# Shared expert and dispatch of a two-layer attention and mixture-of-experts kernel: which TensorE instruction carries the semaphore update of a finished group

## The reference

```python
scores = softmax(xt @ Wg.T)                       # 16 experts
# best 2 of 4 groups of experts, then the best 4 experts of a row
h = silu(einsum('td,eid->eti', xt, W1)) * einsum('td,eid->eti', xt, W3)   # 176 inner
y = einsum('etd,te->td', einsum('eti,edi->etd', h, W2), combine)
z = silu(xt @ Ws1.T) * (xt @ Ws3.T) @ Ws2.T       # shared expert, 352 inner
x = x + y + z
```

## Time and profile before

| | us |
|---|---|
| median of 3 runs | 1459.74 (1458.84 to 1463.13) |
| profiled execution, first to last instruction | 1458.9 |
| PE busy, of the span | 1153.4 (79%) |
| DVE busy | 873.6 (60%) |
| POOL busy | 689.3 (47%) |
| ACT busy | 543.1 (37%) |
| first stage of shared expert and dispatch, about | 386 to 524 |
| the same of the second layer, about | 1096 to 1237 |

### The profile page before, as it was taken

The page is one execution under the profiler, slowest core; times in us unless marked ns, Lnnn a source line. Parts: engine busy times, 40 slices in busy tenths (PEclk is TensorE's granted clock), DMA queues, the critical chain, the costliest instruction groups (busy, mean ns, idle before and its releaser), DMA issues.

```text
span 1458.9 us, 25835 instructions
## 1 busy us (share of the span) xinstructions
PE 1153.4 (79%) x8690; PEld 619.8 (42%) x8690; DVE 873.6 (60%) x2061; ACT 543.1 (37%) x846; POOL 689.3 (47%) x841
## 2 busy tenths in 40 slices
PE   6878999887862399999468899998788227999990
PEld 2333334334631256665244344443275114666650
DVE  5688899853740135555389799998478002455543
ACT  2226677686400012222122477777841001222210
POOL 4443345442067216677563354444502760467771
PEclk9978999999895699999789899999988658999995
DMA  4325556304522148888655321221071322688868
GB/s 150 116 80 180 180 181 191 119 17 147 151 93 106 68 118 152 146 153 147 126 176 166 119 56 55 57 56 32 24 246 38 108 93 78 141 149 150 154 98 248
DMA packets 154353, 177.42 MB, mean 122 GB/s; under 512 B 20016, under 2 KB 139760, under 8 KB 153712
## 3 DMA queue, kind: packets, MB, share of 16 engines
q1 hardware_dynamic: 124336, 136.38, 31.3%
q0 software_dynamic: 29184, 38.36, 15.5%
q10 hardware_dynamic: 704, 1.02, 0.2%
HBM read 91.12 MB, written 83.78 MB: 120 GB/s over the span
## 4 chain that ended last, share of the span: by engine, by line
PE 55%; DVE 18%; another core or an unknown queue 7%; issue 7%; ACT 5%; DMA 4%; SPq 3%; POOL 1%; POOLq 0%; ACTq 0%; DVEq 0%
PE pair_ps L1963 11%; PE o_ps L1734 7%; DVE nm L1103 4%; PE pair_ps L1996 4%; ACT arena L829 3%; DVE bm L1103 3%; PE pair_ps L1999 2%; PE pair_ps L1906 2%; PE t_ps L1760 2%; PE pair_ps L1684 2%; PE pair_ps L1565 2%; PE pair_ps L1970 2%; DMA arena<-mT 2%; PE pair_ps L1659 2%
## 5 line engine op out<-in xcount | busy, mean ns | idle before, releaser
L829 ACT ACTIVATE arena<-pair_ps 128x1024 f32<-128x1024 f32 x320 | 323.4, 1024 | 137.4 <-PE pair_ps L1659 80.2
L614 POOL TENSOR_SCALAR_AFFINE_SELECT arena<-arena 128x512 f32<-128x512 f32 (+1 forms) x320 | 175.7, 549 | 249.0 <-ACT arena L829 248.5
L1103 DVE TENSOR_REDUCE nm<-pair_ps 128x2 f32<-128x1024 f32 (+1 forms) x192 | 232.6, 1222 | 40.4 <-PE pair_ps L1708 36.9
L672 POOL DMA_INDIRECT x_slots<-y_sb,slot_i x128 | 123.3, 963 | 154.0 <-DVE slot_i L1310 115.6
L1734 PE MATMUL o_ps<-arena 128*9 128x512 f32 (+7 forms) x2048 | 179.5, 446 | 4.3 <-POOL arena L614 4.1
L688 POOL DMA_INDIRECT y_h<-xnT,dest x80 | 124.7, 1559 | 107.6 <-DVE xnT L1453 83.6
L688 POOL DMA_INDIRECT y_f<-xnT,dest x80 | 125.0, 1562 | 105.5 <-DVE xnT L1453 80.4
L1963 PE MATMUL pair_ps<-arena 128*128 x512 | 167.0, 467 | 3.1 <-issue 1.7
L1103 DVE TENSOR_REDUCE bm<-pair_ps 128x8 f32<-128x1024 f32 x128 | 155.3, 1217 | 5.7 <-PE pair_ps L1708 2.7
L1916 PE MATMUL t_ps<-arena,hw 128*128 128x256 f32 (+1 forms) x96 | 30.2, 443 | 123.4 <-DVE x_sb L1399 77.5
L1436 DVE TENSOR_TENSOR arena<-arena,pair_ps 128x128 f32<-128x128 f32 x144 | 41.5, 288 | 127.4 <-ACT arena L885 88.1
(11 more groups left out here) (273 smaller groups left out, 2078.5 us busy)
## 6 DMA issues: line engine op xcount, KB each, us to landing
arena<-x_slots SPq DMA_DIRECT2D x128, 132.5 KB
arena<-in_w SPq DMA_DIRECT2D x4, 2816.0 KB, 18.8
x_slots<-hw SPq DMA_DIRECT2D x19, 530.0 KB, 3.6
arena<-q_a SPq DMA_DIRECT2D x64, 96.0 KB
arena<-q_b SPq DMA_DIRECT2D x64, 96.0 KB
y_f<-hw SPq DMA_DIRECT2D x11, 512.0 KB, 4.1
y_h<-hw SPq DMA_DIRECT2D x11, 512.0 KB, 4.1
arena<-in_w SPq DMA_DIRECT2D x2, 2048.0 KB, 17.1
```

What stands on the lines that cost most here:

```text
L614: pool.affine_select(p, p, pattern, ALU.is_ge, 0.0, base=0, channel_multiplier=-1)\
L672: pool.indirect_dma_start(x_slots, bass.IndirectOffsetOnAxis(ap=slot_i[:, t, k:k + 1], axis=0), y_sb[:, t, :], None).then_inc(sm("scat0" i ...
L829: act.activation(p_ring[:, U % RING, :], pair_ps[:, pair_at("T", n, u)].rearrange("p a c -> p (a c)"), ACT.Exp, scale=SCALE).then_inc(sm(" ...
L1103: dve.tensor_reduce(dst, src, X, ALU.max, negate=not 2 <= u < 4).then_inc(sm("t_max_done"), 1)
```

## The change

At four places of `pe_ffn` the semaphore update is taken off the last matmul of a group and put on a drain instruction that is issued right behind it on the same engine: `scan`, `spread`, `shared_in` and `shared_out`. A drain waits until its engine has finished what was issued ahead of it, and makes its update then. That is 12 + 12 + 1 + 1 = 26 drains in each mixture of experts, 52 in all. No product, wait, value or place in an engine's list changes otherwise. `counts`, whose code stands between these, keeps its update on the matmul, and so do the experts.

```diff
             def scan():
                 pe.wait_ge(sm("e_full"), 1 + past(f, 1))
-                pe.matmul(s_ps[:, 1, 0:1], upper, full[:], start=True, stop=True, skip_group_check=True)\
-                    .then_inc(sm("e_scan"), 1)
+                pe.matmul(s_ps[:, 1, 0:1], upper, full[:], start=True, stop=True, skip_group_check=True)
+                pe.drain().then_inc(sm("e_scan"), 1)
...
                 pe.matmul(ps[:, :, NJ:NP], ones, place1[:, :, MIXED:2 * MIXED], start=False, stop=True,
-                          skip_group_check=True)\
-                    .then_inc(sm("e_spread"), 1)
+                          skip_group_check=True)
+                pe.drain().then_inc(sm("e_spread"), 1)
...
             def shared_in(k):
...
-                        mm = pe.matmul(st_ps[0:m, k % 2, 512 * a:512 * a + 512], ws13[:, a, e, r:r + m],
-                                       xnT_all[:, e, b * T:(b + 1) * T], start=e == 0, stop=e == CE - 1)
-                mm.then_inc(sm("e_h"), 1)
+                        pe.matmul(st_ps[0:m, k % 2, 512 * a:512 * a + 512], ws13[:, a, e, r:r + m],
+                                  xnT_all[:, e, b * T:(b + 1) * T], start=e == 0, stop=e == CE - 1)
+                pe.drain().then_inc(sm("e_h"), 1)
...
             def shared_out(k):
...
-                    mm = pe.matmul((t_ps if u < 2 else o_ps)[:, (u % 2) * E:(u % 2) * E + E],
-                                   hw[0:m, k % 2, u * P:(u + 1) * P], ws2[0:m, c, :],
-                                   start=c == 0 and u % 2 == 0, stop=c == 2, skip_group_check=True)
-                mm.then_inc(sm(f + "_hw_used"), 1)
+                    pe.matmul((t_ps if u < 2 else o_ps)[:, (u % 2) * E:(u % 2) * E + E],
+                              hw[0:m, k % 2, u * P:(u + 1) * P], ws2[0:m, c, :],
+                              start=c == 0 and u % 2 == 0, stop=c == 2, skip_group_check=True)
+                pe.drain().then_inc(sm(f + "_hw_used"), 1)
```

## The result

The changed kernel takes **1473.23 us** (median of 3 runs, 1472.01 to 1475.13) against 1459.74 before: ratio 1.0084, 95% interval 1.0058 to 1.0111. It is slower by 0.8%, above the range's upper end of 1470. Its profiled execution has a span of 1473.4 us, 14.5 more than before, at nearly the same mean granted clock (0.901 against 0.898).

What follows compares the result with a forecast made beforehand. PE's semaphore updates, late under POOL's scatters, were taken to bound the kernel. Gains of 34 and 36 us in the two layers, 70 us, off the profiled 1458.9 give 1388.9, forecast as 1390 with the median 0.8 above; range 1345 to 1470.

Steps and rivals of the forecast that it cites:

- What bounds the kernel: Dispatch: PE's updates come up to 67.1 us late under POOL's scatters, leaving 25.9 us of shared expert before the experts.
- everything prompt: Rival: the experts' updates are not held either, so experts start 58 us early in each layer; 1347, chance 0.12.
- The price of a drain: Between PE's matmul groups, a drain costs 0.35 us: a matmul tail of 0.16 plus a weight load of 0.19.
- If a drain's update arrives promptly, nothing holds PE at 426.67: After spread in the first layer, PE runs on and ends the shared expert by 464 with drains, under the scatters.
- The main case: Shared expert hidden under the scatters, experts start 34 and 36 us earlier in the two layers: 70 us, 1390, chance 0.50.
- half: Rival: drains prompter but not prompt, part of the leftover shared expert stays behind the scatters; half of 70, 1425, chance 0.12.
- Drains hold PE: Rival: each drain stops PE until its late update leaves, 9.4 us a layer plus some 4 for clock; 1483, chance 0.11.
- Drains change nothing in the timing, and cost: Rival: updates stay as late, ten drains a layer stand in the open behind the scatters, 7 us; 1467, chance 0.15.

Runs made afterwards that it cites:

- e14: Kernel before, with POOL waiting after every eighth scatter until all so far have landed; chip with late completions: 1376.57 us, ratio 0.9406.
- e16: Kernel before, with POOL pausing after every 16th scatter only; chip with late completions: 1433.43 us, ratio 0.981.
- e17: Kernel before, with POOL pausing after every 12th scatter; chip with late completions: 1402.64 us, ratio 0.960.
- e13: Kernel before, with drains only behind the last product of scan and of spread, two a layer; chip with late completions: 1465.03 us, ratio 1.0016.
- e12: Kernel before, with drains only behind shared_in 8 to 11 and shared_out 6 to 11, ten a layer; chip with late completions: 1468.58 us, ratio 1.0033.
- e11: The changed kernel with all 52 drains, measured again against the kernel before; chip with late completions: 1475.79 us, ratio 1.0075.
- e9: Kernel before, with drains only behind scan and spread; chip with prompt completions: 1342.12 us, ratio 1.0004.
- e1: Kernel before, with drains only behind scan and spread, four in the run; chip with prompt completions: 1341.33 us, ratio 1.0010.
- e2: Kernel before, with drains only behind shared_in from piece 8 and shared_out from piece 6; chip with prompt completions: 1342.15 us, ratio 1.0013.
- e10: Kernel before, with drains only behind shared_in from piece 8 and shared_out from piece 6; chip with prompt completions: 1341.30 us, ratio 1.0004.
- e15: The changed kernel with all drains, plus POOL's pause after every eighth scatter; chip with late completions: 1370.91 us, ratio 0.939 to the kernel before.

## Why the prediction was wrong

**What bounds the kernel: right.** Completions late by up to 67 us under the scatters are behind the 50.39 us and the work left over. Two measurements stand behind it: with the pauses they vanish and 86 us with them, and on a prompt chip the unchanged kernel takes 1341. My rival "everything prompt" priced just that at 1347, within 0.5%; its own 58 us a layer make 116 and not the 113 that I took off, so 1344, which is nearer still. And that the experts' own scatters, which don't run back to back, do no such harm fits e14, e16 and e17.

**The price of a drain: right.** 0.35 us was taken. Behind the scatters in the changed kernel, pieces follow in steps of 5.85 us (Silus at 508.06 and 513.91) where 5.16 was the pace before: 0.69 for two drains, 0.35 each.

**"If a drain's update arrives promptly, nothing holds PE at 426.67": this step failed.** I had shown that the update came 64.9 us behind the matmul's end, and that end is modelled. From it I took that the matmul was done and only its message was late, so that another messenger would be prompt. That PE began out(5) at 441.14 speaks for the first half; no row stood behind the second. e13 shows that a drain behind that matmul is released when a matmul's own update comes, 0.14 us apart in one trace: what is late is completion as the sequencer sees it, whoever carries it. `order()` moved from 491.64 to 492.81 and not to 430. Everything behind this step, 70 us, fell with it.

The rule of the Trainium skill that I had weighed, "PSUM — Partial Sum Buffer", section "Engine vs sequencer instructions", says that updates on an engine's instruction fire on its completion and that a drain waits for the engine to go fully idle. From it I now take that a drain can't come earlier than the matmul's update. I had written that the trace disagrees. It did not: 64.9 us was measured against a modelled end, and e13's drain (64.1 us) agrees with the rule.

**The main case (0.50) and "everything prompt" (0.12), "half" (0.12)** all stood on that step. So three quarters of the chance rested on one assumption, and I had counted it as several cases.

**"Drains hold PE" (0.11): the mechanism and its main term were right.** It was priced at 9.4 us a layer: out(5) and in(7) moved behind the scatters, 5.2, and 12 exposed drains, 4.2; and some 4 us of a colder clock for both layers. All three came.

The shared expert's work behind the scatters took 25.85 us before (496.71 to 522.56) and 37.02 after (492.76 to 529.78), 11.2 longer, and in the second layer 26.05 and 37.07, 11.0 longer. Of that the clock took 2.1 and 1.9: out(5) and in(7) ran 9.53 us (9.58) at a granted clock of 0.50 at first (1.2 GHz, the lower of its two levels), where the next piece with its drains took 5.85, while before the same slow start cost out(6) only 1.6 (1.8). With 5.2 for the two groups, 3.9 is left for the drains, in each layer. The mean clock of the whole run (0.901 against 0.898) hides this.

What the rival did not have is that this work began 1.2 and 3.2 us sooner behind the first scatter than before; so D grew by 9.95 and 7.88 only. That it met 9.4 so closely is in part luck. Another 2.7 us came back in front of the first scatters, where the kernels that are alike in that stretch differ by up to 5.7 us (e12 401.41, e16 407.11). 1483 was forecast, 1473.23 measured.

The parts on the late chip, by the ratios: scan and spread 2.3, last pieces 4.8, and 3.9 of the 11.0 left to the drains between. The intervals allow 0 to 8 for this last one, and D leaves nothing for it: 10.5 and 6.4 make 16.9, and e11 has 16.8.

The range ended at 1470 because this case was left out of it. Its argument against, that PE's waits for others end promptly, spoke of arrivals at PE and said nothing of completions.

**"Drains change nothing in the timing, and cost", 1467,** is about where the time would lie had PE not stood. e12 has just the drains of that case, and its ratio of 1.0033 gives 1464.6 on the prediction's chip: 4.8 us for the 7 that were forecast.

**What stays open.** Why some chips show it and others not; which unit serves completions late (the scatters' own data is not late: their last DMA packets end some 2.06 us behind a scatter's start, in the kernel before and after and in e9 alike); and what about a gap cures it, its length, landing or POOL's rest.

One thing goes with the lateness in every trace: records of semaphore updates are missing. The first 40 scatters raise `scat0` 16 times each, 640 in all. The traces of the prompt chips hold all 640 in the first layer, the kernel before 108, the change 111, e13 94, e16 135, e14 234; the last one recorded comes 51.8 us behind the first scatter before and 52.0 in e9, so those that are there are not late. This points at the path of semaphore updates or of their records. Which of the two is crowded, and whether the recording itself takes part in the lateness, no run here tells.

The changed kernel alone was never measured on a prompt chip; e1, e2, e9, e10 and e15 make "no difference" likely there, which is argued and not shown.

## What to carry to other kernels

When an update comes long after its matmul, the recorded end of the matmul is no proof that it was done: before moving the update to another instruction, ask what would be late if completion itself is, because a drain then turns a wait of others into a stop of TensorE. Look at what runs without a gap in the same stretch and give it one: a wait after every eighth scatter was worth 6% here on chips with late completions, and cost 1.4% on the others. A drain costs about 0.35 us between float32 groups where TensorE bounds the stretch, and nothing under cover.

## What the runs showed of the hardware

The same program takes 1341 us on two chips (or in two sessions), and 1460 to 1463 us on three others and in the runs of the prediction. The difference arises in the two stretches of scattering: D is 61 and 64 us shorter on a prompt chip (58.4 and 58.2 in e9), 125 us together, of which some 7 are lost again in the rest. On the slower chips TensorE's completions, matmuls' and drains' alike, are late from some 12 us into a gapless run of indirect DMAs by GpSimd, each 0.96 us with 0.30 between; in the changed kernel PE's groups are released at 437.03, 458.73 and 481.12, some 22 us apart. VectorE's and ScalarE's completions are prompt in the same stretch (ACT ends at 440.36 and DVE starts at 440.40), and so are the DMAs' landings (as recorded, 51.8 us against 52.0 for the 40th). A gap of 1.86 us after every 8 of them prevents it, after 12 or 16 only in part. A speed measured on one chip says little of another here: with pauses of eight the kernel is the best on one kind, and on the other behind the unchanged one.
